# A narrow attention step with two maxima issued as a pair, feed-forward stages begun in another order, and a quantised product whose normalisation is applied behind it, half by half

## The reference, cut to what matters

```python
x = x + tanh(g_xattn[0]) * L0_attention(layernorm(x), ctx)      # 16 heads of 8 features, softmax ("narrow")
x = x + tanh(g_ffn[0])   * L0_experts(layernorm(x))             # F0: products with running sums, routed by softmax
x = x + tanh(g_xattn[1]) * L1_attention(layernorm(x), ctx)      # 16 heads of 64 features, squared relu ("wide")
x = x + tanh(g_ffn[1])   * L1_experts(layernorm(x))             # F1: one expert of 8 per token
x = x + tanh(g_xattn[2]) * L2_attention(layernorm(x), ctx, ctx) # 16 heads of 8, softmax, no projections ("narrow")
x = x + tanh(g_ffn[2])   * (layernorm(x) @ (int4(kernel) + a @ b) + bias)   # the quantised product
x = x + tanh(g_xattn[3]) * L3_attention(layernorm(x), ctx)      # 16 heads of 64, softmax, clipped ("wide")
x = x + tanh(g_ffn[3])   * L3_experts(layernorm(x))             # F3: two experts of 8 per token, and a shared one

def layernorm(x): return (x - mean(x)) / sqrt(var(x) + 1e-5)
```

## Time and profile before

| | us |
|---|---|
| median of 3 runs | 834.1 |
| the profiled execution | 834.92 |
| its span in the trace | 833.1 |
| PE busy | 779.5 (94% of the span) |
| DVE busy | 606.3 (73%) |
| ACT busy | 452.3 (54%) |
| POOL busy | 192.1 (23%) |

### The profile page before, as it was taken

How to read it: one execution, slowest core, us unless ns; L and a number is a source line. 1 busy time by engine, 2 the same in 40 slices (tenths; PEclk the granted TensorE clock), 3 DMA queues, 4 the chain that set the end, 5 groups by cost and what they waited for, 6 DMA issues and landing times. The chain is left out here.

```text
span 833.1 us, 14405 instructions
## 1 busy us (share of the span) xinstructions
PE 779.5 (94%) x5298; PEld 561.8 (67%) x5298; DVE 606.3 (73%) x1157; ACT 452.3 (54%) x681; POOL 192.1 (23%) x160
## 2 busy tenths in 40 slices
PE   5999789989999999999989997899998899999998
PEld 4655456656677686777776555666775767777776
DVE  6688676767766577888776887776655887788875
ACT  3477442146655416999924775466554165555553
POOL 3000100024646420232320001146466101111111
PEclk9999979989999998999999999999999999999999
DMA  9100000220221200000270000002302000000000
GB/s 349 74 2 2 1 1 0 80 124 1 54 46 33 52 2 0 1 0 1 101 322 1 2 2 1 2 2 52 78 1 53 1 0 1 0 1 0 1 0 26
DMA packets 3950, 30.56 MB, mean 37 GB/s; under 512 B 593, under 2 KB 945, under 8 KB 2353
## 3 DMA queue, kind: packets, MB, share of 16 engines
q1 hardware_dynamic: 3888, 29.73, 10.7%
HBM read 29.10 MB, written 0.62 MB: 36 GB/s over the span
## 5 line engine op out<-in xcount | busy, mean ns | idle before, releaser
L187 PE MATMUL banks<-normed_t_high,work_split 128*128 128x512 f32 x250 | 109.7, 439 | 8.4 <-DVE work_split L1183 3.6
L1120 POOL TENSOR_TENSOR work<-work 128x512 f32<-128x512 f32 x64 | 86.2, 1354 | 120.9 <-ACT work L1082 120.8
L737 DVE TENSOR_REDUCE work<-banks 128x2 f32<-128x512 f32 x128 | 84.4, 688 | 30.1 <-PE banks L457 18.6
L189 PE MATMUL banks<-normed_t_high,work_split 128*128 128x512 f32 x250 | 100.7, 403 | 0.0
L188 PE MATMUL banks<-normed_t_low,work_split 128*128 128x512 f32 x250 | 100.5, 402 | 0.0
L1919 ACT ACTIVATE work<-banks 128x512 f32<-128x512 f32 x68 | 40.6, 598 | 72.5 <-PE banks L189 72.5
L187 PE MATMUL banks<-work_split 128*128 128x512 f32 (+1 forms) x160 | 66.7, 417 | 4.6 <-DVE work_split L1997 2.9
L2030 DVE TENSOR_TENSOR work<-work,banks 128x512 f32<-128x512 f32 x68 | 46.7, 687 | 32.0 <-ACT work L1919 31.3
L187 PEld LDWEIGHTS banks<-normed_t_high,work_split 128*128 128x128 f32 x250 | 47.8, 191 | 30.2 <-issue 16.4
L940 PE MATMUL banks<-work 128*64 128x256 f32 x512 | 65.3, 394 | 2.7 <-ACT work L1082 2.2
L1762 DVE TENSOR_TENSOR work_split<-work,work_split 128x512 fp32r<-128x512 f32 x64 | 52.0, 814 | 17.7 <-ACT work_split L1684 17.3
(11 more groups left out here) (299 smaller groups left out, 1752.9 us busy)
## 6 DMA issues: line engine op xcount, KB each, us to landing
raw_b<-in_wf SPq DMA_DIRECT2D x1, 6528.0 KB, 18.0
raw_a<-in_wf SPq DMA_DIRECT2D x1, 4096.0 KB, 12.1
raw_b<-reciprocal_rows SPq DMA_DIRECT2D x6, 512.0 KB, 5.8
raw_a<-reciprocal_rows SPq DMA_DIRECT2D x6, 512.0 KB, 5.8
raw_a<-in_wf SPq DMA_DIRECT2D x1, 2048.0 KB, 14.7
raw_b<-in_wb SPq DMA_DIRECT2D x1, 2048.0 KB, 19.0
raw_a<-in_wb SPq DMA_DIRECT2D x1, 2048.0 KB, 8.1
small_operands<-in_small SPq DMA_DIRECT2D x1, 1386.0 KB, 10.5
```

The source lines that it names most:

```text
L187: nc.tensor.matmul(o, w[0], m[0], start=start, stop=False)
L189: return nc.tensor.matmul(o, w[1], m[0], start=False, stop=stop)
L737: nc.vector.tensor_reduce(a_nm[:, t:t + 2, j], bank(7 - n % 2).rearrange("p (e k) -> p e k", e=2), AX.X, ALU.max, negate=True).then_inc(A[ ...
L1120: nc.gpsimd.tensor_tensor(w_ps[g % 2].rearrange("p (h q) -> p h q", h=2), v[:, :, 0, :], v[:, :, 1, :], ALU.add).then_inc(W["ps"].sem, 1)
```

## The change: what it does, and the diff

Four parts.

1. **Narrow step** (both attentions). The maxima 4 and 5 are issued as a pair once DVE has taken the first four, with the scores of unit 2 behind them. `next_rows(0)` stands ahead of that pair, `next_rows(1)` behind those scores. ACT's copy of the first rows stands ahead of its third exponential.
2. **Feed-forward heads.** F0: both first products ahead of the transposes of the router's stack, ACT's copy of the stack behind its first two others, and the experts' biases ahead of the last two `out`. F1: the first two `up` ahead of the logits, waiting for the first half only; DVE's and ACT's router work behind two steps.
3. **Second junction.** The layer norm ahead of the quantised product is not made on tokens. The raw residual is transposed (`raw_half_pe`), multiplied with the weights less their column means (`quant_centre_pe` makes them once), and the row's factor times the gate is applied when the product is added to the residual (`quant_half`). Half 0 does this inside the last slot of the attention, half 1 behind it. The low part of the context moves from DVE to POOL.
4. **Start of the wide attention.** ACT's copies of the first values stand ahead of the copies of the normalised tokens (both). In layer 3 half 0 is projected and scored before half 1 is projected.

```diff
@@ narrow attention, PE and ACT
-                more(4)
-                more(5, 2)
                 next_rows(0)
+                maxima_pair(x + 1, 4)
+                scores_ready(x, 2)
+                scores(x, 2, 0, 1)
+                next_rows(1)
                 more(6, 3)
                 more(7)
-                next_rows(1)
                 values(x, 0)
                 if x + 2 < STEPS:
-                    first_maxima(x + 2)
+                    maxima_pair(x + 2, 0)
@@ last slot, PE, c = 1
+                    raw_half_pe(pe, 0)
                 values(x, 0)
+                    quant_half_pe(pe, 0)
                 values(x, 1)
@@ f0_pe
+                    if n == 2 and not ahead:
+                        biases()
                     out(i, n)
...
             products(0, 0)
+            products(0, 1)
             stack_pe(pe, 0)
-            products(0, 1)
@@ f1_pe
-            logits_pe(xf, col("centroids"), 5, ready=2 * m + 1)
...
-            pe.wait_ge(s_xs, 2 * splits(m) + 2)
+            pe.wait_ge(s_xs, 2 * splits(m) + 1)
             up(0, 0)
             up(0, 1)
+            logits_pe(xf, col("centroids"), 5, ready=2 * m + 1)
+            pe.wait_ge(s_xs, 2 * splits(m) + 2)
@@ quantised product
+        def raw_half_pe(pe, h):
+            pe.wait_ge(s_ra, h + 1)
+            for t in range(4 * h, 4 * h + 4):
+                last = nc.tensor.transpose(ps[:, 7 - 2 * h, (t % 4) * P:(t % 4 + 1) * P], res[:, t, :], ident)
+            last.then_inc(s_xt, 1)
+        def quant_half_pe(pe, h):
+            pe.wait_ge(s_qc, 1)
+            pe.wait_ge(s_xf, 2 * 5 + h + 1)
+            tokens_half(xf, q_c[:, :], h)
+        def quant_half(dve, order, h):
+            norm_factors(dve, order, 5, h)
+            at = slice(4 * h, 4 * h + 4)
+            order.step(nc.vector.tensor_scalar(q_g[:, at], Z[0].rs[:, at], gate[:, 5:6], None, ALU.mult))
+            dve.wait_ge(s_rt, 2 * 3 + h + 1)
+            for t in range(4 * h, 4 * h + 4):
+                order.done(nc.vector.scalar_tensor_tensor(out=res[:, t, :], in0=ps[:, 6 + h, (t % 4) * P:(t % 4 + 1) * P],
+                                                          scalar=q_g[:, t:t + 1], in1=res[:, t, :],
+                                                          op0=ALU.mult, op1=ALU.add))
+            order.wait()
@@ start of the wide attention, PE, c = 1
+                norm_half_pe(pe, n, 0)
+                stream(7, 6)
+                pe.wait_ge(s_xs, 2 * splits(m) + 1)
+                project(0)
+                norm_half_pe(pe, n, 1)
             at("va", 2)
             scores(0)
             at("va", 4)
             scores(1)
...
+                stream(6, 4)
+                pe.wait_ge(s_xs, 2 * splits(m) + 2)
+                project(1)
@@ start of the wide attention, ACT
+            norm(0)
+            if c == 0:
+                norm(1)
             high(0)
+            if c == 1:
+                norm(1)
             high(1)
             weights(0)
@@ POOL
+            norm_half_pool(pool, 5, 0)
+            norm_half_pool(pool, 5, 1)
+            context_low(pool, 0)
+            norm_half_pool(pool, 6, 0)
+            context_low(pool, 1)
+            norm_half_pool(pool, 6, 1)
```

More of the change, by code:

```diff
@@ L297, in norm_pe @@
             for h in range(2):
[L298 to L303, removed]
-            for h in range(2):
[L306 to L312, removed]
-                    ins = nc.scalar.activation(half(high, h), bank(k + h), ACT.Copy)
-                ins.then_inc(s_xf, 1)
@@ new lines, in norm_act, with norm_half_act @@
+        def norm_act(act, m, f32=True, high=None, w=None, b=None, k=6):
+            for h in range(2):
+                norm_half_act(act, m, h, f32, high, w, b, k)
+        def norm_half_act(act, m, h, f32=True, high=None, w=None, b=None, k=4):
+            act.wait_ge(s_xt, 2 * m + h + 1)
+            act.wait_ge(s_xs, 2 * splits(m))
+            if f32 and w is None:
+                ins = nc.scalar.activation(half(xf, h), bank(k + h), ACT.Copy)
+            elif f32:
+                ins = nc.scalar.activation(half(xf, h), bank(k + h), ACT.Identity, bias=b, scale=w)
+            if high is not None:
+                ins = nc.scalar.activation(half(high, h), bank(k + h), ACT.Copy)
+            ins.then_inc(s_xf, 1)
@@ new lines, in norm_dve_split, with norm_half_split @@
+        def norm_dve_split(dve, order, m, hi, lo, from_bank=True, k=6, between=None):
+            for h in range(2):
+                if h == 1 and between is not None:
+                    between()
+                norm_half_split(dve, order, m, h, hi, lo, from_bank, k)
+        def norm_half_split(dve, order, m, h, hi, lo, from_bank=True, k=4):
+            dve.wait_ge(s_xf, 2 * m + h + 1)
+            src = bank(k + h) if from_bank else half(xf, h)
+            if not from_bank:
+                order.step(nc.vector.tensor_copy(half(hi, h), src))
+            nc.vector.tensor_tensor(half(lo, h), src, half(hi, h).bitcast(F32), ALU.subtract).then_inc(s_xs, 1)
@@ L1475, in f0_pe @@
             f0_passes(pe, body)
-            for h in range(2):
-                nc.tensor.matmul(bank(6 + h), col("b_experts"), half(f_wt, h).bitcast(F32), start=False, stop=True)\
-                    .then_inc(s_fb, 1)
             tokens_pe(pe, out_t, col("W_O"), ((s_fo, 1), (s_fq, 1)))
@@ L2145, in _ @@
             f0_act(act)
-            norm_act(act, 2, f32=False, high=xh, k=4)
-            wide_act(act, 0, ACT.Square, col("nbias"))
+            for h in range(2):
+                wide_first_tiles_act(act, 0, h)
+            wide_act(act, 0, ACT.Square, col("nbias"), lambda h: norm_half_act(act, 2, h, f32=False, high=xh))
             norm_act(act, 3, high=xh)
```

270 lines of the change are left out of this document (164 added, 106 removed).

## The result

The changed kernel takes 828.6 us, the median of 21 runs (824.7 to 836.7), beside 834.1 for the kernel before on the same chip. The ratio is 0.9942, 95% interval 0.9917 to 0.9967: faster, by about 5 us. The forecast was 828.0 with 824 to 832.5.

A forecast was written before the change was run, and what follows sets the result against it. Narrow slots were taken as a loop through PE and DVE, the second junction as bound by its chain. Terms summed to -6.2 us: 834.9 to 828.7 profiled, 827.9 median, stated as 828; 8-in-10 range 824 to 832.5.

The forecast's parts named there:

- Narrow step: Narrow attention slots: reordered maxima and rows make ten slots 0.19 us shorter each; with the ends, -1.0 us together.
- the ends: Slots x = 0 and x = 6 of both narrow attentions: the pair only waits, +0.2 and +0.25, twice, +0.9 us.
- Rival B: Narrow slots close to DVE's need: 0.3 us more in ten slots, 3 us, giving 825 us; chance 0.12.
- F0's end: End of F0: biases ahead of the last two `out` let the output product start sooner, -0.9 us.
- F0's start: Start of F0: router's stack and second products change places; gain only if PE gets the fast clock sooner, -0.4 us.
- Value copies: ACT's value copies ahead of the normalised tokens fill a wait; first `high` sooner, -0.2 us in layer 1.
- New operations: One centring on DVE, one product and one copy at the second narrow attention's start: +0.3 us.
- F1's start: Head of F1: first `up` begin some 2 us sooner; between -1.7 and +0.5 us, taken as -0.3.
- Second junction: Last division to first projection 5.5 us shorter, wide start 1.8 us longer: net -3.7 us.
- Rival A: Second junction's gain held up by POOL: two holds of 1.5 us on DVE, giving 831 us; chance 0.20.
- Rival C: Clock falls in the narrow slots, about 1.3 us per fall; from eight falls on, over 4 us slower; chance 0.06.
- Rival D: The change does nothing, the junction's chain being held by ACT rather than DVE: about 834 us; chance 0.12.

The follow-up runs named there:

- e8: Changed kernel with the pair of maxima 4 and 5 directly behind the transposes of the sums, first and second rows behind it, in every narrow slot: 830.5 us, ratio 0.9948.
- e1: Kernel before with only the narrow slots changed: median 831.5 us, ratio 0.9954.
- e4: Kernel before with narrow slots, F0 and F1 changed, without the second junction and the wide starts: ratio 0.9899.
- e3: Kernel before with only the head of F1 changed: median 830.3 us, ratio 0.9945.
- e6: Changed kernel with 2 and 2 fillers instead of 6 and 6 ahead of the transposes of the second junction's first normalised half: 825.7 us, ratio 0.987.
- e2: Kernel before with only the two changes of F0: median 833.3 us, ratio 0.9988.
- e10: Same kernel as e4, run again in a second series: median 827.2 us, ratio 0.9925.
- e12: Kernel of e11 with the context's two low parts on DVE instead of POOL: median 823.4 us, ratio 0.9857.
- e11: Changed kernel with the second wide attention's first two exponentials ahead of the second high, and the fewer fillers of e6: median 831.9 us, ratio 0.9862.

## Why the prediction was right, and where it was not

**The total** was right by compensation and by luck: two terms were far off in opposite directions, and at the same clock the change is worth 4.2 ±0.5 us, where the sum has 6.2. Chance in the clock and in the medians of 21 runs brought the result the rest of the way.

**Narrow step, -1.0: 4.3 ±0.8 measured, a mis-sized term.** The walk's mechanism holds. From the pair of maxima 4 and 5 to the next first pair I had 3.35 us, the rows give 3.31 (473.34 to 476.65), and the first rows take 0.64 instead of 0.66. What failed is the step that I did not walk: I let PE reach the end of the transposes when it did before. But full-width rows start 0.41 us behind the start of those transposes (472.29 to 472.70), where a 32-row maximum started 0.59 behind in before:

```profile
470.76 0.66 PE L525 MATMUL banks<-small_operands,work 128*128 128x128 f32 x4
471.35 0.87 PE L457 MATMUL banks<-work_split 32*128 32x256 f32 x3
```

That is 0.18 of the missing 0.23 per slot, read from rows alone: e8, meant to test it, held its maximum for DVE, 1.02 behind (471.56 to 472.58). And the ends, +0.9, come to about +0.15 by e1 and e4 (-0.13 and +0.2, twice). Ten slots by -0.42 and these ends are -4.05. Rival B had the right size with the wrong reason: PE is still busy for 7.19 of 7.38, DVE for 6.59, so the slot did not close to DVE's need.

**F0's end, -0.9: right**, -0.99. **F0's start, -0.4:** not shown. **Value copies, -0.2:** 0.7 less at layer 1's fourth projection (13.45 against 14.2 us). **New operations, +0.3:** from F1's first weighing to the first transposes of the narrow slots it takes 111.2 to 111.5 us with them and without, so nothing that shows.

**F1's start, -0.3: wrong in kind.** I gave one value in a range of -1.7 to +0.5. It has two: -0.8 and +1.9, by whether the clock rises while the logits run or five us behind them. At the same clock e3 gains nothing; its better median is the clock's.

**Second junction, -3.7: 0.1 ±0.8 measured, mis-sized in all of its terms.** The delay of the last division is 1.5 by order (1.3 forecast), and 0.9 more, put down to a fall of the clock. From there 14.97 us (13.3 forecast): L240 held by POOL 0.96, transposes behind fillers 1.1. Without the fillers and without that hold (e6, 13.83 less 0.96) 12.87 us are left, which is the sum of rows I had (12.8), with none of the 0.5 for waits. The wide start takes 15.2, forecast 14.8. At the fast clock the parts give +1.5 - 5.1 + 2.2 = -1.4; the low clock in the last slots leaves -0.5 of it in the trace. Why whole runs at the same mean clock show not even that is open. Of that clock: in before, e1 and e2 some 3 us at 1.2 GHz lie between 484 and 509 and 3 between 509 and 530 (e3 and e4 have none and 3, e10 has 7 and 3); in the eight profiles with the new junction there are 7 or 10 in the first stretch and none in the second.

**The rule on the shared ports** ("SBUF — State Buffer", section "SBUF: two separate sides", of the Trainium skill) spoke against the change, and the runs agree: 1.13 against 0.17 for one row, gone in e12. I had put the holds on the additions that read a bank, which keep their 1.13, and priced two holds of 1.5; it was one of 0.96, on a step of four elements per row. Rival A was right in kind and a third of its size. The prediction had named POOL on the junction's chain as a sign that it is wrong, and that sign is there; it cost 1 us of a total that came out all the same.

**Rival C**, a clock that falls in the steady slots, is refuted for the steady slots: their window has 1.00, and in all fourteen profiles the falls within a narrow attention lie in its first two slots or at its end. In the second slot the changed profile does have low clock that before lacks (453 to 457), which the prediction had excluded. At the end the clock goes to and fro, 0.76 over 79 to 93 us with two falls, with PE busy for 12.7 of the 14; in before the same window has 1.00 with PE busy for 11.7. The Trainium skill ("TensorE: Matmul & The Clock Gate", section "HAM oscillation — how this bites in real kernels") tells of such a to and fro where PE waits for data between bursts. The trace agrees on the effect; that waits bring it about here it does not show, since before waited more in this window. **Rival D** came true of the junction in whole runs, but not for its reason: the chain itself got 5.1 us shorter up to the first projection.

## What to carry to other kernels

Take stages apart before believing a sum: here the right total hid a term four times too small and another that was worth next to nothing. When an order on an engine is changed, look at which kind of instruction now follows which, and at every instruction that stands ready behind one that waits; both big surprises, the slot and ACT's exponentials, were of these kinds. And where the granted clock varies from run to run, compare times at one clock, and count how long each stage stays at the low level over several profiles.

## What the runs showed of the hardware

- 0.01 of mean granted clock is worth 6.1 us of some 830, with 1.3 us of scatter left. One kernel's runs go from 0.965 to 0.987 (e11), so the mean of 12 runs moves by 2 to 3 us on that account alone.
- The same order of F1's head gives two lengths, 18.0 or 20.8 us, and hardly anything between; the old order gives 18.9 each time.
- From the start of four 128x128 transposes a full-width product (128*128) begins after 0.41 us, a 32-row product (32*128) after 0.59 and, in the same slots, the values (128*32) after 0.59 too (477.09 to 477.68).
- A DVE operation on 128x4 elements took 1.13 us instead of 0.17 beside a POOL operation on two tensors, while bank-reading additions beside POOL's next one kept 1.13 for four.
